# The expert output turned in another bank, a norm bias on GpSimd, and a new order in an eight-layer kernel

## The reference

```
x = x + layernorm(layer(layernorm(x)))
```

```
routing = softmax(xf @ router_w.T + router_b)
sel_w, sel_idx = top_k(routing, 2);  sel_w = sel_w / sel_w.sum()
shared_out = ffn(xf, shared_w1, shared_b1, shared_w2, shared_b2)   # w2 . gelu(w1 x + b1) + b2
acc = sum over experts of comb[:, e] * ffn(xf, spec_w1[e], ...)
out = shared_out + acc
```

## Time and profile before

| | |
|---|---|
| median of 3 runs | 1497.29 us (1494.82 to 1498.85) |
| profiled execution, own time | 1497.26 us |
| its span | 1495.5 us |
| mean granted clock of TensorE | 0.873 |
| TensorE busy | 1153.5 us, 77% |
| VectorE busy | 1011.6 us, 68% |
| ScalarE busy | 736.1 us, 49% |
| GpSimd busy | 613.0 us, 41% |

### The profile page before, as it was taken

How to read it: one execution, slowest core, us unless ns; L and a number is a source line. 1 busy time by engine, 2 the same in 40 slices (tenths; PEclk the granted TensorE clock), 3 DMA queues, 4 the chain that set the end, 5 groups by cost and what they waited for, 6 DMA issues and landing times.

```text
span 1495.5 us, 13396 instructions
## 1 busy us (share of the span) xinstructions
PE 1153.5 (77%) x3922; PEld 576.7 (39%) x3922; DVE 1011.6 (68%) x2234; ACT 736.1 (49%) x1396; POOL 613.0 (41%) x422
## 2 busy tenths in 40 slices
...
DMA packets 11272, 17.77 MB, mean 12 GB/s; under 512 B 1304, under 2 KB 7584, under 8 KB 10688
## 3 DMA queue, kind: packets, MB, share of 16 engines
...
## 4 chain that ended last, share of the span: by engine, by line
PE 39%; DVE 10%; ACT 5%; issue 3%; POOL 2%; POOLq 0%; DVEq 0%; ACTq 0%
PE bankE L1862 6%; PE bankE L1248 4%; PE bankS L1779 2%; PE bankE L1779 2%; PE bankE L1310 2%; PE bankS L1810 2%; PE bankS L1825 1%; PE bankS L1782 1%; PE bankE L1269 1%; PE bankE L623 1%; PE bankE L1782 1%; PE bankS L1752 1%; PE bankE L582 1%; ACT b_pr L1146 1%; PE bankE L545 1%
## 5 line engine op out<-in xcount | busy, mean ns | idle before, releaser
L753 DVE TENSOR_TENSOR_SCAN hs<-dA,carry,bankS 128x512 f32<-128x512 f32 x128 | 156.6, 1264 | 2.8 <-ACT dA L396 0.5
L331 POOL TENSOR_TENSOR hc<-hs,cb 128x1024 f32<-128x1024 f32 x56 | 131.8, 2353 | 60.5 <-DVE hs L753 58.0
L308 POOL TENSOR_TENSOR cv<-cv,hc 128x1024 f32<-128x1024 f32 x56 | 132.8, 2371 | 4.4
L1737 ACT ACTIVATE c_h<-bankE,C 128x512 f32<-128x512 f32 x144 | 98.7, 687 | 63.7 <-PE bankE L1862 61.2
L1631 POOL TENSOR_TENSOR c_acc<-c_acc,c_tw 128x512 f32<-128x512 f32 x32 | 45.3, 1415 | 178.2 <-DVE c_tw L1955 178.2
L446 ACT ACTIVATE sg<-bankE,C 128x512 f32<-128x512 f32 x80 | 54.4, 687 | 97.2 <-PE bankE L582 96.9
L1862 PE MATMUL bankE<-c_fH,c_w1H 128*128 128x512 f32 x144 | 83.7, 581 | 1.1 <-ACT c_h L1737 1.1
L745 DVE TENSOR_TENSOR bankS<-dx,bankS 128x1024 f32<-128x1024 f32 x64 | 78.4, 1225 | 7.8 <-PE bankS L511 7.1
L545 PE MATMUL bankE<-h2T,wg 128*128 128x512 f32 x128 | 75.9, 677 | 10.0 <-ACT wb L457 7.5
L396 ACT ACTIVATE dA<-dl,Aneg 128x512 f32<-128x512 f32 x128 | 80.9, 709 | 3.1 <-DVE dl L736 3.0
L623 PE MATMUL bankE<-hh,f 128*128 128x512 f32 x128 | 68.9, 620 | 7.3 <-DVE hh L867 7.3
...
## 6 DMA issues: line engine op xcount, KB each, us to landing
...
```

The costliest lines, as they stand in the source:

```text
L308: pool.tensor_tensor(cv[:, :, :], cv[:, :, :], (hv if by_vector(i, k) else hc)[:, :, :], ALU.add).then_inc(s["y_acc"], 1)
L331: pool.tensor_tensor(dst[:, :, :], hs[:, k % HS, :, :], cb[:, k % 2, :].unsqueeze(1).to_broadcast([P, HV, G]), ALU.mult).then_inc(s["hc_re ...
L753: V.tensor_tensor_scan(hs[:, k % HS, h, :], dA[:, (HV * k + q) % DA, :], dbx[:, h, :], carry[:, k, h:h + 1], ALU.mult, ALU.add).then_inc(s ...
L1737: act.activation(h[:, n % 3, :], E[k % 2][:, :], ACT.Gelu_apprx_tanh, bias=col("b1_3", k)).then_inc(s["fs_ready"], 1)
```

## The change

Three edits. First, the last layer's output turn goes to `OUT[i > 0]`: for the first group the routing bank E[3] as before, for the other three S[0], and the wait and the reader of E[3] are registered for the first group alone. Second, the bias nbE: VectorE makes nmE=-mean in piece L4 ahead of the variance, and GpSimd multiplies it by rsE right behind its power, in the same piece; piece L5 has no part on VectorE any more. Third, the list `ORDER` is sorted anew; nearly all of its lines differ, and one of before and two of after stand here.

```diff
 ORDER = [(p[0], p[1:].split(".")[0], int(p.split(".")[1])) for p in """
...
-    cR2.2 cy1.1 cW1.1 cU28.1 cU29.1 cU30.1 cU31.1 cU32.1 cU33.1 cR3.2 cs3.0 cU34.1 cU35.1 cV1.1 cU0.2 cU1.2 cO0.1 cs4.0 cU2.2 cU3.2 cO1.1
+    cW1.1 cV1.1 cR2.2 cU28.1 cU29.1 cs2.0 cU30.1 cX1.1 cU31.1 cU32.1 cU33.1 cR3.2 cU34.1 cs3.0 cU35.1 cU0.2 cU1.2 cO0.1 cs4.0 cU2.2 cU3.2
+    cO1.1 cs5.0 cs6.0 cU4.2 cU5.2 cU6.2 cO2.1 cU7.2 cU8.2 cU9.2 cU10.2 cU11.2 cU12.2 cU13.2 cU14.2 cU15.2 cU16.2 cR0.3 cs7.0 cU17.2 cU18.2
...
     XA = sb2("XA", [P, 2 * T * P])
     stE, mvE = sb2("stE", [P, T, 6]), sb2("mvE", [P, T, 2])
-    powE, rsE, nbE = sb2("powE", [P, 3, T]), sb2("rsE", [P, 3, T]), sb2("nbE", [P, T])
+    powE, rsE, nbE, nmE = sb2("powE", [P, 3, T]), sb2("rsE", [P, 3, T]), sb2("nbE", [P, T]), sb2("nmE", [P, T])
...
             elif p == "L4":
                 power("e_var", "e_pow", powE, rsE, e, 1, 3)
+                at_least(pool, s["e_pow"], e, 3, 2)
+                pool.tensor_tensor(nbE[:, :], nmE[:, :], rsE[:, 1, :], ALU.mult).then_inc(s["nb_ready"], 1)
...
                 stats(lambda j: X[:, cols(e, j)], stE, mvE, chain2)
+                inc2(V.tensor_scalar(nmE[:, :], mvE[:, :, 0], -1.0, None, ALU.mult))
                 ask("e_var", 1, mvE, powE, LN_EPS)
-            elif p == "L5":
-                at_least(V, s["e_pow"], e, 3, 2)
-                V.scalar_tensor_tensor(nbE[:, :], mvE[:, :, 0], -1.0, rsE[:, 1, :], ALU.mult, ALU.mult).then_inc(s["nb_ready"], 1)
...
     DOWN = (E[2], S[3])
+    OUT = (E[3], S[0])
...
             elif p == "O1":
                 pe.wait_ge(s["c_acc"], (NX - 1) * (i + 1))
-                e3_next(s["c_done"], i + 1)
-                turn(E[3], acc_of(NX - 1)).then_inc(s["moT_ready"], 1)
+                if i == 0:
+                    e3_next(s["c_done"], 1)
+                turn(OUT[i > 0], acc_of(NX - 1)).then_inc(s["moT_ready"], 1)
...
             elif p == "O1":
                 dve.wait_ge(s["moT_ready"], 2 * NG + i + 1)
-                stats(tj(E[3]), stO, mvO)
+                stats(tj(OUT[i > 0]), stO, mvO)
                 dve.tensor_scalar(powO[:, :], mvO[:, :, 1], LN_EPS, None, ALU.add).then_inc(s["f_var"], 1)
             elif p == "O2":
-                norm(tj(E[3]), tj(xnO), None, nO, mvO, rsO, "f_pow")
+                norm(tj(OUT[i > 0]), tj(xnO), None, nO, mvO, rsO, "f_pow")
```

More of the change, by code:

```diff
@@ new lines @@
+    aN9.0 aA7.0 an9.0 ao9.0 aN10.0 an10.0 ao10.0 aN11.0 an11.0 ao11.0 aN12.0 an12.0 ao12.0 aN13.0 an13.0 ao13.0 aN14.0 an14.0 ao14.0 aN15.0
+    an15.0 ao15.0 aB1.0 aB3.0 aB4.0 aB2.0 aF1.1 aF5.1 aM0.0 aF6.1 aF2.1 aF0.1 aF7.1 aM1.0 aF3.1 aF8.1 aF4.1 aR1.0 aF9.1 aA0.1 aR3.0 aA1.1
+    aR4.0 aN0.1 an0.1 aM2.0 ao0.1 aN1.1 aM3.0 an1.1 aM4.0 aA2.1 ao1.1 aN2.1 an2.1 aM5.0 ao2.1 aM6.0 aA3.1 aN3.1 an3.1 aM7.0 ao3.1 aN4.1
+    aM8.0 an4.1 aM9.0 ao4.1 aN5.1 aM10.0 an5.1 aM11.0 ao5.1 aN6.1 aM12.0 an6.1 aM13.0 ao6.1 aN7.1 an7.1 aM14.0 ao7.1 aM15.0 aA4.1 aA5.1
@@ new lines @@
+    aA6.1 aL1.0 aL3.0 aA7.1 aN8.1 aL4.0 an8.1 ao8.1 aL5.0 aN9.1 an9.1 aR2.0 ao9.1 aU0.0 aN10.1 an10.1 aU1.0 aU2.0 ao10.1 aU3.0 aR5.0 aN11.1
+    an11.1 ao11.1 aR6.0 aN12.1 aU4.0 an12.1 aU5.0 ao12.1 aN13.1 aU6.0 an13.1 aU7.0 ao13.1 aN14.1 aU8.0 an14.1 aU9.0 ao14.1 aN15.1 aU10.0
+    an15.1 aU11.0 aU12.0 aU13.0 ao15.1 aB1.1 aU14.0 aB3.1 aU15.0 aB4.1 aU16.0 aB2.1 aF1.2 aU17.0 aF5.2 aU18.0 aF6.2 aU19.0 aF2.2 aF0.2 aL2.0
+    aF7.2 aL6.0 aF3.2 aF8.2 aF4.2 aF9.2 aA0.2 aL7.0 aR1.1 aA1.2 aA2.2 aR3.1 aN0.2 an0.2 aM0.1 ao0.2 aR4.1 aN1.2 aM1.1 an1.2 aM2.1 aM3.1
```

79 lines of the change are left out of this document (35 added, 44 removed).

## The result

The changed kernel took 1473.41 us (median of 4, 1470.81 to 1474.89) against 1496.05 for the one before: ratio 0.9852, 95% interval 0.9830 to 0.9874, so 22 us faster, where 15.2 were forecast and 1475 was the low end of the range. In a second comparison it was 0.9864 (0.9846 to 0.9882), 20 us. The profiled execution took 1474.89, its span is 1473.1; by the two traces the last instruction of the fourth group comes 22.4 us earlier.

A forecast was written before the change was run, and what follows sets the result against it. TensorE was taken as full before the tail, with some 20 us idle in it, waiting. Gains of 9.2 (bank), 5.0 (nbE) and 1.0 (order) made 15.2 off 1497.26: 1482 us, 8-in-10 range 1475 to 1493.

The forecast's parts named there:

- part 3: The newly sorted instruction list, whole kernel: three places could matter, counted together as 1.0 us gained.
- Part 1: Last layer: the next group's weight spread no longer waits for the output turn's bank; 9.2 us gained, bounds 7.7 to 10.4.
- What I deducted for VectorE's load: Last layer, group 3: 4.5 us taken of 5.7 at most, as VectorE is nearly the limit, 59.6 busy of 76.
- Rival A: Last layer: VectorE becomes the limit and TensorE waits for c_hL instead; 1490.8 us, chance 0.14.
- Rival B: Last layer: something else holds the spread at U7 for as long; 1490.3 us, chance 0.05.
- Part 2: nbE made on GpSimd: 1.9 us earlier in three cases, 0.2 later in a fourth; 5.0 gained, bounds 0 to 6.3.
- The rule that I cited against the change: Shared ports go to whichever instruction starts first, so VectorE could hold GpSimd's new small multiply in turn.
- the 0.7 that I derived for the whole part: The nbE edit's gain in us if a 128x1024 VectorE instruction held GpSimd's small multiply.
- Part 3 (a): Entry to mamba stages: R3 and R4 moved behind F9 delay the first scan; counted 0, bounds -2 to +4.7 a stage.
- rival C: Mamba stages: R3 and R4 delay the first scan, 5.0 us a stage, 15.0 in three; 1503.1 us, chance 0.08.
- Part 3 (b): wkv stage: K2 moved ahead into VectorE's idle time before a product; 1 us gained, bounds 0 to 3.
- Part 3 (c): Exponentials A4 to A7 and last attention pieces placed elsewhere, some behind the X matmuls; 0, bounds -2 to +2.

The follow-up runs named there:

- e2b: Kernel before with only nbE multiplied on GpSimd, old order and bank, repeated for its trace; the same code measured 0.9974 of the kernel before.
- e4: Kernel before with the output bank and nbE edits together, old order; 0.9942 of the kernel before, 8.7 us faster.
- e1: Kernel before with the output bank alone changed, old order and nbE on VectorE; 0.9954 of the kernel before, 6.9 us faster.
- e7: Changed kernel with the old order from list place 425 to the end (wkv, attention, last experts); 0.9868 of the kernel before.
- e8: Changed kernel with nbE back on VectorE, new bank and new order kept; 0.9901 of the kernel before.
- a1: The changed kernel itself, run again as a yardstick; 0.9864 of the kernel before.
- e6: Changed kernel with the old order in list places 0 to 309 (mamba groups 1 to 3, experts 1 and 2); 0.9887 of the kernel before.
- e5: Changed kernel with the old order in list places 309 to 425, from the fourth mamba group's projections; 0.9915 of the kernel before.
- e10: Changed kernel with the old order in list places 309 to 342 alone, in the fourth mamba group; 0.9895 of the kernel before.
- e3: Kernel before with the new order list alone, old bank and nbE on VectorE; 0.9962 of the kernel before, 5.7 us faster.
- e12: Changed kernel with R1's norm three tiles ahead in group 4 and the old order in list places 722 to 845; 0.9832 of the kernel before, median 1469.38 us.

## Why the prediction was wrong

Bank and bias gave about what was forecast; the new order, counted at nearly nothing, gave as much as the bank. The three edits in all eight combinations, in us against before (ratio times 1495; each by about 2.4 either way): bank -6.9, nbE -3.9, order -5.7, bank and nbE -8.7, bank and order -14.8, nbE and order -7.6, all -21 (mean of two comparisons). The difference that an edit makes, averaged over the four states of the other two, is 8.6 for the bank, 3.5 for nbE, 7.5 for the order. Forecast were 9.2, 5.0 and 1.0. The sum failed at part 3, the order.

- **Part 1, the bank: right.** The stages show 4.5 in group 4 (4.7 forecast) and 6.1 in group 3 in the new order (4.5 taken; the upper bound was 5.7) or 1.3 (e2b to e4) to 4 (e1) in the old. What I deducted for VectorE's load didn't arise, as X1.1 was gone from behind O2: where it stands there still, TensorE waits 2.84 (e1, e4) or 1.71 (e7) for c_hL, in the changed kernel 0.55. Rival A's waits for c_hL stayed at 0.55 and 1.11; VectorE's load shows in the wait for the norm of R1 alone, 4.80 for 3.75. Rival B is refuted by the row at 1415.53.
- **Part 2, nbE: the mechanism right, the count of places wrong.** The collision is real (2.29 on VectorE, 0.20 on GpSimd in its place) and the small multiply was held only in the wkv stage. But I multiplied 1.9 by three as if the order stayed. In the new order two of three collisions are gone without the edit (e8). What it gains there is 3.5 in one stage, as ScalarE's chain waits 4.19 for that one, less 1.1 in wkv; by time the edit is worth 5.5 there, and the trace has 2.4 of that in the rest of lane b, in which the two kernels have the same code. The rule that I cited against the change (the Trainium skill, "SBUF — State Buffer", "SBUF: two separate sides": whichever instruction starts first keeps the ports, VectorE's too) came true in the fourth place, where I had counted 0.2: the trace agrees with it in which engine waits, with the power at 1.91 for 1.01 and the multiply at 0.51 for 0.20. The page has the other engine block fully; here the power lost 0.9 of the 1.11 us that the scan still had to run. In the three mamba places it didn't arise, so the 0.7 that I derived from it for the whole part was too low.
- **Part 3 (a), the order at 0: the step that failed.** I priced only what it costs, the late first scan, and wrote off the earlier M chain as something that "may give something back". The first scan of group 2 did come late: from the end of F9 to that of n0 it takes 10.7 us in place of 3.8. But F9 itself ends sooner, as R3 and R4 are gone from F (149.53 in place of 155.39), and counted from B2 of the first group the first scan ends after 37.8 (changed) or 40.1 us (a1), against 36.5 before and 34.7 in e6: 1.3 to 5.4 later, my bound being 4.7. Of rival C's 5 us a stage nothing like it arrives at the end: g2 is 155.7 to 160.8 in the new order, 157.5 to 159.0 before, g3 shorter or 1.0 longer, M 5 shorter, and the old start is 3.4 slower by time (e6), so rival C is refuted. The order, counted at nothing here and at 1 in all, was worth 7.5 on the mean and some 12 on top of the other edits. 7.6 of these sit in one stretch (e5): 4.1 are the M pieces and R4 moved ahead of the scans in the fourth group (e10), 3.4 the regrouped powers, L and R pieces (e5 less e10). R4's last instruction no longer begins inside a 128x1024 instruction of GpSimd (2.87 to 0.68) and starts 2.6 sooner, R5's no longer either (2.36 to 0.42).
- **Part 3 (b): right in sign, small in size.** wkv gives 1.7 with nbE changed (e7 to the changed kernel: 124.8 to 123.1) and 2.7 to 3.3 without (e8 and e3 against before), for 1 counted.
- **Part 3 (c): wrong.** I gave the attention pieces a bound of 2 either way and took 0; they cost 2.4 to 2.8 in att (before and e12 against the changed kernel), with the 3.50 wait inside the X matmuls. By time the 2.8 isn't shown by itself.

Left open: whether the surplus of all three together (21 against the 16.5 of the three alone, and against some 14.6 from singles and pairs) is more than chance, since each term is uncertain by 2.4; the stages explain 2.1 of it in last 3 (the wait of 2.84 behind X1.1, which only the bank and the order together take away) and the rest not. Also where e6's 3.4 come from: its trace puts the loss into stages of the same code at a lower clock. The second group's 155.8 to 160.8 with the same code are TensorE's clock, as the windows above show; what decides when it rises isn't shown.
